# ScalarE normalises a group's output between later exponentials, and VectorE adds one probability tile more in the third block of groups 1 to 3

## The reference

```python
qkv = x @ Wqkv.T + b            # 16 query heads of 32, one key head and one value head shared by all
attn = softmax(causal(q @ k.T * 32**-0.5))
x = layernorm(x + (attn @ v) @ out_w.T + out_b)
s = x @ router_w.T              # 8 experts, top 2, softmax over the two scores
h = silu(xb @ w1[e]) * (xb @ w3[e])     # bfloat16, FF = 128
x = layernorm(x + sum over the top two e of gate[e] * (h @ w2[e]))
```

## Time and profile before

| | before |
|---|---|
| median of 3 runs | 1118.79 us (1118.54 to 1118.96) |
| the profiled execution's own time | 1121.4 us |
| span of the profiled execution | 1119.7 us |
| mean granted TensorE clock | 0.993 |
| PE busy | 1079.0 us (96%) |
| DVE busy | 888.6 us (79%) |
| ACT busy | 713.4 us (64%) |
| POOL busy | 199.3 us (18%) |

### The profile page before, as it was taken

One profiled execution on the slowest core, in us unless ns is written; L12 is line 12 of the kernel. 1 busy time (PEld: TensorE's weight loads), 2 busy tenths in 40 slices (PEclk: granted clock), 3 DMA queues, 4 the chain that ended last, 5 costly groups with the idle time before them and its releaser, 6 DMA issues.

```text
span 1119.7 us, 17340 instructions
## 1 busy us (share of the span) xinstructions
PE 1079.0 (96%) x5970; PEld 520.2 (46%) x5994; DVE 888.6 (79%) x1101; ACT 713.4 (64%) x844; POOL 199.3 (18%) x162
## 2 busy tenths in 40 slices
PE   8999999999999999999989999999999999999996
PEld 6365435543337433335634643474333654333462
DVE  4566899779976699987667679976998767898956
ACT  6734785478864498885445457644888447888821
POOL 3520332013110120111032013301211201211000
PEclk9999999999999999999989999999999999999999
DMA  4976401442001622001352353016400152200001
GB/s 146 208 114 141 124 1 40 106 121 38 2 2 53 137 76 38 1 1 39 78 136 75 75 131 76 2 52 138 113 1 1 39 126 65 38 1 2 1 1 38
DMA packets 40331, 72.19 MB, mean 64 GB/s; under 512 B 13969, under 2 KB 14993, under 8 KB 40209
## 3 DMA queue, kind: packets, MB, share of 16 engines
q1 hardware_dynamic: 24624, 56.64, 19.1%
q0 software_dynamic: 13584, 11.54, 7.1%
q10 hardware_dynamic: 2000, 2.51, 0.7%
HBM read 25.58 MB, written 8.39 MB: 30 GB/s over the span
## 4 chain that ended last, share of the span: by engine, by line
PE 75%; DVE 12%; issue 5%; ACT 2%; POOL 2%; DMA 1%; SPq 1%; DVEq 0%; ACTq 0%; POOLq 0%
PE sc L1184 21%; PE bank L1206 19%; PE sc L1037 8%; PE bank L1037 7%; PE sc L1327 7%; DVE psum_k L833 5%; PE sc L1224 3%; PE sc L1342 2%; PE bank L1224 2%; DVE stats L909 2%; POOL prob L520 1%; DVE res L906 1%; PE bank L1335 1%; PE sc L1271 1%; PE bank L1342 1%
## 5 line engine op out<-in xcount | busy, mean ns | idle before, releaser
L653 ACT ACTIVATE prob<-sc 128x1024 f32<-128x1024 f32 x544 | 525.5, 1025 | 133.7 <-PE sc L1184 133.5
L833 DVE TENSOR_TENSOR psum_k<-psum_k,prob 128x2048 f32<-128x2048 f32 x170 | 403.4, 2373 | 4.7
L1184 PE MATMUL sc<-q_st,k_st 128*128 128x512 f32 x1088 | 327.1, 422 | 8.0 <-DVE rden L882 3.8
L1184 PEld LDWEIGHTS sc<-q_st,k_st 128*128 128x128 f32 x1088 | 183.7, 188 | 249.7 <-ACT prob L653 177.3
L1206 PE MATMUL bank<-prob,v_sb 128*32 128x512 f32 x2176 | 288.2, 607 | 3.3 <-POOL prob L520 3.3
L520 POOL TENSOR_SCALAR_AFFINE_SELECT prob<-prob 128x1024 f32<-128x1024 f32 x64 | 112.4, 1798 | 527.7 <-ACT prob L653 527.7
L1327 PE MATMUL sc<-prob,w_sb 128*128 128x512 bf16 x503 | 117.3, 379 | 1.3 <-issue 1.3
L1206 PEld LDWEIGHTS bank<-prob,v_sb 128*32 128x32 f32 x2176 | 44.5, 108 | 107.4 <-issue 89.4
L683 ACT ACTIVATE prob<-sc 128x512 f32<-128x512 f32 x64 | 38.0, 594 | 73.0 <-PE sc L1327 72.9
L833 DVE TENSOR_TENSOR psum_k<-prob 128x2048 f32<-128x2048 f32 x28 | 64.0, 2286 | 20.7 <-POOL prob L520 17.1
L1037 PE MATMUL bank<-q_st,wq_hi 128*128 128x512 f32 x240 | 80.3, 399 | 0.0
(11 more groups left out here) (160 smaller groups left out, 1017.5 us busy)
## 6 DMA issues: line engine op xcount, KB each, us to landing
q_st<-q_hi SPq DMA_DIRECT2D x120, 128.0 KB, 2.4
q_st<-q_lo SPq DMA_DIRECT2D x120, 128.0 KB, 2.4
res<-in_x SPq DMA_DIRECT2D x8, 1024.0 KB, 5.3
res<-ob_sb POOLq DMA_DIRECT2D x8, 1024.0 KB, 9.5
out_x<-res SPq DMA_DIRECT2D x32, 256.0 KB, 2.1
res<-in_xT SPq DMA_DIRECT2D x7, 1024.0 KB, 5.0
w_sb<-in_w POOLq DMA_DIRECT2D x8, 256.0 KB, 9.1
prob<-in_wqkvT ACTq DMA_DIRECT2D x4, 288.0 KB, 6.1
```

The costliest lines, as they stand in the source:

```text
L653: nc.scalar.activation(prob[t % NP][:, half * HW:(half + 1) * HW], score_half(q // TB, 2 * t + half).rearrange("p m n -> p (m n)"), ACT.Ex ...
L833: nc.vector.tensor_tensor(acc[:, :], first[:, :], prob[t % NP][:, :], ALU.add).then_inc(add_v, 1)
L1184: last = nc.tensor.matmul(dst, k_st[:, k * P:(k + 1) * P], q_st[slot][:, c * HJ:(c + 1) * HJ, at:at + P], start=True, stop=not shift)
```

## The change

The output of groups 0, 1 and 2 is no longer normalised by VectorE. POOL makes a second per-token factor after rstd, `nmr` = -mean * rstd, in two small instructions, and ACT computes rstd * x + nmr in place, one token tile behind each of the exponentials number 8, 9, 10 and 11 of the next group. Group 3 of each sequence is normalised as before. VectorE's next write of `mv` waits for `nmr`, and POOL's next write of rstd waits for ACT's four instructions.

BY_PE falls by one for q = 6 (1 to 0), q = 10 and q = 14 (2 to 1): VectorE adds one tile more there, and PE has one part less. All other blocks keep theirs.

```diff
+OUT_LAG = 8
-BY_PE = [0] + [1] * 9 + [2] * (NQ - 10)
+BY_PE = [0, 1, 1, 1] + [1, 1, 0, 1] + [1, 1, 1, 2] + [2, 2, 1, 2]
...
+                def make_nmr(g):
+
+                    pool.wait_ge(rstd_ready, count(b, rstd_ready, 2 * g + 2))
+                    pool.sem_inc(waited_apart, 1)
+                    nc.gpsimd.tensor_scalar(nmr[:, :], mv[:, :, 0], -1.0, None, ALU.mult).then_inc(nmean_ready, 1)
+                    pool.wait_ge(nmean_ready, count(b, nmean_ready, g + 1))
+                    pool.sem_inc(waited_apart, 1)
+                    nc.gpsimd.tensor_tensor(out=nmr[:, :], in0=nmr[:, :], in1=rstd[:, :],
+                                            op=ALU.mult).then_inc(nmr_ready, 1)
...
                         if q == TB * g and g:
                             make_rstd(2 * g)
+                            make_nmr(g - 1)
...
+                    if g:
+                        pool.wait_ge(out_ready, count(b, out_ready, TB * g))
+                        pool.sem_inc(waited_apart, 1)
                     make_rstd(2 * g + 1)
...
+                def normalise_out(g, t):
+                    act.wait_ge(nmr_ready, count(b, nmr_ready, g + 1))
+                    r = res[g % 2][:, t, :]
+                    nc.scalar.activation(r, r, ACT.Identity, bias=nmr[:, t:t + 1],
+                                         scale=rstd[:, t:t + 1]).then_inc(out_ready, 1)
...
                         exp_tile(t)
+                        if g and OUT_LAG <= t - FIRST[TB * g] < OUT_LAG + TB:
+                            normalise_out(g - 1, t - FIRST[TB * g] - OUT_LAG)
...
                 def finish_attention(g):
 
+                    if g:
+                        dve.wait_ge(nmr_ready, count(b, nmr_ready, g))
...
-                    normalise(g, 2 * g + 2, out_ready)
+                    if g == NG - 1:
+                        normalise(g, 2 * g + 2, out_ready)
```

More of the change, by code:

```diff
@@ L187, in build @@
         rstd = sb("rstd", [P, TB])
+        nmr = sb("nmr", [P, TB])
         rsc = sb("rsc", [P, TB, E])
@@ L289, in build @@
         rstd_ready = sem("rstd_ready")
+        nmean_ready = sem("nmean_ready")
+        nmr_ready = sem("nmr_ready")
         x1_ready = sem("x1_ready")
@@ L335, in build @@
             biased: 16 * NG, outproj: TB * NG, resid1: TB * NG, mv_ready: 2 * NG, eps_in: 2 * NG,
-            rstd_ready: 2 * NG, x1_ready: TB * NG, x1_turned: TB * NG, x1T_ready: TB * NG,
+            rstd_ready: 2 * NG, nmean_ready: NG - 1, nmr_ready: NG - 1, x1_ready: TB * NG, x1_turned: TB * NG, x1T_ready: TB * NG,
             x1Tb_ready: TB * NG, routed: NG, dtop_ready: NG, etop_ready: NG, ghl_ready: NG,
```

## The result

| | before | after |
|---|---|---|
| median of 16 runs each, same chip | 1118.88 us (1116.46 to 1121.68) | 1121.12 us (1119.3 to 1123.61) |
| ratio, after to before | | 1.0019 [1.0011, 1.0027] |
| profiled execution: own time, span | 1121.4, 1119.7 us | 1122.1, 1120.4 us |

The change makes the kernel slower by 0.19% (2.1 us), with an interval of 0.11% to 0.27%. That is a small loss whose point value lies just inside the 0.2% called "no change" in the prediction. The forecast was +0.6 us; the loss is 1.6 us larger than that.

A forecast was written before the change was run, and what follows sets the result against it. PE, busy 96% of the span, was taken as the bound. A sequence sums +2.0 - 1.2 + 0.15 - 1.15 + 0.5 = +0.3 us, +0.6 for both: 1119.4 us against the median of 1118.79, range 1114.3 to 1123.5.

The forecast's parts named there:

- Block 6, +2.0: Group 1: the new add delays VectorE's split and transpose, scores start 1.8 us later, plus 0.2 allowed at `xT_lo`: +2.0 a sequence.
- the slot: Block 6: the scores need the slot of the denominators' transpose, which ends at 170.74, so they start at 170.8, not 169.02.
- The removed normalisation: Start of groups 1 to 3: VectorE begins adds up to 3.4 us earlier; gain 0.7 and 0.5 us a sequence.
- The waits before block 8's denominators and for block 13's mask: Groups 2 and 3: PE's waits of 0.69 us for VectorE's last add and 0.46 us for POOL's mask were to go.
- The 1.5 us "given back" to POOL: Start of groups 1 to 3: four small POOL instructions beside adds give back perhaps 1.5 us of VectorE's earlier start.
- Blocks 10 and 14: Groups 2 and 3: the scores needing the transpose start earlier despite the new add, -1.2 and -1.15 us a sequence.
- the mis-sized term: ACT's new instructions make PE wait 0 us in group 1, 0.15 in group 2 and 0.5 in group 3, a sequence.
- 0.74, or 0.64 between starts: ACT's new instruction with two per-token operands: its length and start distance in us, with bounds 0.53 and 0.9.
- the prediction's estimate by it: By the skill's rule ACT's instruction takes 0.80 us, 0.71 between starts; some 1 us more over the launch.
- (a), hidden adds: Block 6's denominators are read as early as before, group 1 turns to -0.9: 1113.7, or 1111.4 without ACT waits; chance 0.17.
- (b), `xT_lo` ahead of the last add: Ends of groups 1 and 3: VectorE's last add waits 4.6 us, about 4.1 lost each time: 1123.5 to over 1130; chance 0.12.
- (c), ACT at 0.9: Groups 1 to 3: ACT's instruction at 0.9 us between starts costs 6.8 us over the launch: 1124.9; chance 0.11.

The follow-up runs named there:

- kernel 1: The kernel before with only the three added adds (blocks 6, 10 and 14), VectorE still normalising the output: 1121.14 us, ratio 1.0032.
- Kernel 3: The changed kernel with block 6's part back on PE, blocks 10 and 14 as in the change: 1120.19 us, ratio 1.0023.
- kernel 6: The changed kernel with ACT's four instructions as copies with immediate operands, the output not normalised, half of the input stored: 1117.79 us, one run.
- Kernel 4: The changed kernel with ACT's four instructions behind exponentials 8, 11, 14 and 17 instead of 8 to 11: 1117.51 us, ratio 0.9999.
- 5: The changed kernel with ACT's instructions behind exponentials 8, 11, 14, 17 and block 6's add moved to blocks 4, 8 and 12: 1118.88 us, ratio 1.0.
- 7: Kernel 3 with 40 instead of 24 idle transposes at the start of PE's program: 1119.83 us, ratio 1.0011.
- 2: The changed kernel with the old list of sums, so only the normalisation is moved to ACT: 1118.93 us, ratio 1.0011.
- kernel 8: The kernel before with 40 instead of 24 idle transposes at the start of PE's program: 1120.0 us, ratio 1.0014.
- 9: The changed kernel with ACT's instructions spread, added adds only at blocks 10, 12 and 14, and 16 instead of 24 idle transposes: 1113.63 us, ratio 0.9962.
- 10: The same as 9 with 12 idle transposes instead of 16: 1118.18 us, ratio 0.9996.

## Why the prediction was right, and where its terms were off

**Block 6, +2.0: right in place and size, and in part by luck in the changed kernel.** The new add makes VectorE late, and PE waits for the slot: the first add of block 7 at 165.66 (165.5 forecast), the transpose at 170.18 (170.03), group 1 +2.03 and +1.47 us and, in the first sequence, +0.39 in the stage behind it. The order is not the one worked out. The prediction had the mask end at 162.85 as before, the new add wait for it and the split cost 0.61; kernel 1 shows just that. In the changed kernel the mask came 0.28 us later than before, just too late to be ahead of an add. So the new add ran ahead of the mask's second half, which ended at 165.19, the split waited again (1.57), and the sum came out the same. For this reason PE waited twice, 0.79 for the mask and 1.56 for the transpose, instead of once for 2.6. The one long wait of kernel 1 cost half-clock time as well; the two short ones did not. The forecast foresaw neither; that the order came out this way spared the change the clock's price. Kernel 3, with only this edit taken back, has neither wait.

**The removed normalisation: right where it counted.** VectorE's first add of group 1 starts at 121.80 in the changed kernel, 3.1 us earlier, and the lead ends at block 4's transpose as said (135.55; 135.53 in the earlier trace rows). The waits before block 8's denominators and for block 13's mask are gone. The 1.5 us "given back" to POOL were wrong in direction: VectorE gives nothing, POOL waits. VectorE and then POOL at the start of group 1:

```profile
121.80 2.29 DVE L859 TENSOR_TENSOR psum_k<-prob 128x2048 f32<-128x2048 f32 x1
```

```profile
121.90 2.27 POOL L549 TENSOR_SCALAR rstd<-mv 128x4 f32<-128x4 f32 x1 [6.37 <-DVE mv L936]
124.26 3.05 POOL L551 TENSOR_TENSOR rstd<-rstd,mhalf 128x4 f32<-128x4 f32 x1
127.50 1.34 POOL L558 TENSOR_SCALAR nmr<-mv 128x4 f32<-128x4 f32 x1 [0.20 <-POOL rstd L551]
129.02 0.20 POOL L561 TENSOR_TENSOR nmr<-nmr,rstd 128x4 f32<-128x4 f32 x1 [0.18 <-POOL nmr L558]
```

The first two of them took 0.23 and 1.03 us in the kernel before, with no add in flight:

```profile
121.72 0.23 POOL L545 TENSOR_SCALAR rstd<-mv 128x4 f32<-128x4 f32 x1 [6.07 <-DVE mv L910]
122.03 1.03 POOL L547 TENSOR_TENSOR rstd<-rstd,mhalf 128x4 f32<-128x4 f32 x1
```

The last takes 0.20 us here, as no add is in flight then. By the groups of lines, the 12 new ones take 16.8 us in all, and the 32 that make rstd, which are as many as before, took 25.5 us and take 50.0: nearly all of the 41.7 us on POOL's line of the page are waiting, not work. It cost nothing, because nmr is first needed 8 tiles later.

**Blocks 10 and 14: right in mechanism.** In the changed kernel PE waits behind them for the transpose, shortly, as foretold:

```profile
314.58 1.19 PE L1213 MATMUL sc<-q_st,k_st 128*128 128x512 f32 x4 [0.28 <-DVE rden L908]
...
493.97 1.20 PE L1213 MATMUL sc<-q_st,k_st 128*128 128x512 f32 x4 [0.16 <-DVE rden L908]
```

Of 0.85 us of PE work each (one part less), 0.45 and 0.65 were left (0.5 and 0.65 forecast).

**ACT: the mis-sized term.** The prediction took "0.74, or 0.64 between starts"; the trace has 0.83 and 0.71. PE lost 0.33 us in group 2 (0.15 forecast) and 0.89 in group 3 (0.5, the periods above), 0.57 us more a sequence, 1.1 us over the launch. The step that was mis-sized is the price of an operand. The prediction took it from the distance between the copy (0.63) and an instruction with one operand (0.688), some 55 ns, and added it twice; but the one reads SBUF and the other PSUM, so the distance is not an operand's price alone. In kernel 6 the same instruction without its operands takes 0.654 us, so the two cost 178 ns, or 89 each if they cost the same. The Trainium skill ("ScalarE: Activation LUTs", What ACT_TABLE_LOAD costs) had the better number: the prediction's estimate by it, 0.80 and 0.71 us, and PE waiting 0.35 and 0.8, agrees with this trace within 0.1 us (0.83, 0.71, 0.33 and 0.89). Kernel 4 shows that the loss is one of order, not of work: the same 24 instructions, spread, cost PE nothing that the timeline shows.

**Not foreseen.** (1) +0.84 us (0.16 in the second sequence) at the start of group 3, where PE waits for VectorE's residual:

```profile
389.11 1.67 PE L1213 MATMUL sc<-q_st,k_st 128*128 128x512 f32 x6 [0.78 <-DVE res L932]
```

Kernels 4, 5, 6 and 7 have the wait as well (0.46, 0.76, 0.80 and 0.76 us in the first sequence), kernels 1, 2, 3, 8, 9 and 10 do not. 3 and 7 differ only in idle transposes, so it is no part of what the edit does to attention. It is VectorE's second residual that is late: VectorE is free 0.58 us before it and begins it at 388.36, when PE's last down projection has ended (388.33); in the kernel before it follows without a gap. Why stays open. (2) The stop at 724.73 is gone in the changed kernel (-1.2 us against the forecast). It gave back what (1) cost, by luck: idle transposes alone remove it too, in kernel 8. (3) The clock piece, -1.3 us in one execution. These account for the rest: +0.6 forecast, +1.1 for ACT, +1.0 for (1), -1.2 for (2), and about +0.5 over the remaining stages, which I do not explain, make the 2.0 us without the clock. So the forecast is right as a small change, with block 6's cost and the gains behind it in their places; that the whole stayed near it owes something to errors that cancel.

**The rivals.** (a), hidden adds, did not occur: kernel 1 has block 6's wait without the moved output, and kernel 3, without that add, has none. (b), `xT_lo` ahead of the last add, did not occur: POOL's operation stands at 180.29 with 6.08 us, 0.66 us after the last add began (0.7 forecast), and the split at 181.84 with 5.08; in group 3 the distance is 0.37 (0.3 forecast). (c), ACT at 0.9, lay 0.2 us per instruction too high.

**Still open.** What in PE's code decides where it stops. That stops come and go with nothing but instructions ahead of them is what 3 against 7 and before against 8 show, in one trace of each; whether a stop comes in every execution of a kernel is not shown. 9 against 10 changes the clock of the first microseconds as well. The stop near 62 us has not moved with 16 transposes more or 8 fewer. That PE waits there for its own instructions is inferred from "issue" and from the 16 KB packets on the instruction queue: in the twelve traces, behind the program's start, there are 23 such stops of over 0.5 us, and each time such a packet had ended 1.2 to 2.6 us before PE went on (1.2 to 1.7 in 20 cases; in the other three two packets had run at once). But the packets stand some 3 us apart there and pass without a stop too, and no run changed the loading itself. And the ratios of kernels 3, 5, 7, 8, 9 and 10 hold such stops, so the price of an edit is better read from the stages than from their totals.

## What to carry to other kernels

An add moved from the engine that sets the pace to one that "has time" pays only where that engine isn't at that moment feeding a mask or an eviction: read who is late next at the very place (block 6: nothing gained, 2 us lost; block 12: all gained). Instructions slipped between the exponentials of an engine with 0.3 us of room a tile cost PE 0.33 and 0.89 us a group side by side and nothing three tiles apart. And where a change of under 1% is judged, look in both traces for stops of PE with "issue" and for stretches at half clock: here a stop lengthened its stage by 1 to 3 us and a stretch by 1.7, they come and go when a few instructions are added ahead of them or between two executions, and they can be mistaken for the edit's effect.

## What the runs showed of the hardware

- A 4-column operation on POOL that starts 0.1 us behind VectorE's 2.29 us add lasts 2.27 us, and the next, behind the next add, 3.05 us; without an add in flight they last 0.23 and 1.03 us. VectorE's adds keep their 2.29 us, while VectorE's split waits behind POOL's big operation. Who came second waited here, whatever its size. So 0.1 us can decide a mask's length: 4.18 us for two halves that begin 0.14 us ahead of an add, 6.25 us where they begin 0.09 us behind one. The Trainium skill ("SBUF — State Buffer", SBUF: two separate sides) says of this lock that whichever starts first holds it; by that rule the trace agrees.
- Behind a 2.56 us wait of PE the granted clock fell to half (1.2 GHz) for some 3.4 us in three of four cases of kernels 1 and 6; behind waits of 0.79 and 1.56 us (0.87 and 0.89 for the first in kernel 4), 4 us apart, it did not, in four of four cases of the changed kernel and kernel 4. A wait of 2.56 us can so cost 4.3. A wait of 2.4 us near 580 us, which all twelve traces have, goes with such a fall in ten of them.
- PE can stop for 0.6 to 2.9 us with no semaphore to wait for; 16 idle transposes at the program's start made such stops go and others come.
- Idle transposes at the program's start went with a higher clock behind them: with 24 of them PE's first matmuls take 0.40 us, with 12 they take 0.63 us until 13.5 us. Four of them fewer, with a stop that came and one that went, moved the kernel from 1113.63 to 1118.18 us.
